# Half of the cross-attention probabilities carried through DRAM and transposed in 32x32 blocks by VectorE

## The reference

```python
qh = _split_heads(einsum('bnq,qi->bni', x, Wq))        # (8, 2048, 128)
kh = _split_heads(einsum('bmc,ci->bmi', context, Wk))  # (8, 4096, 128)
vh = _split_heads(einsum('bmc,ci->bmi', context, Wv))
sim = einsum('hid,hjd->hij', qh, kh) * SCALE
mean = mean(sim, axis=-1, keepdims=True)
sim = (sim - mean) * 1.5 + mean
attn = softmax(sim, axis=-1)
out = einsum('hij,hjd->hid', attn, vh)                 # then the heads side by side
return einsum('bni,iq->bnq', out, Wout) + bout
```

## Time and profile before

| | us |
|---|---|
| median of 3 runs | 2606.53 (2606.34 to 2611.48) |
| span of the profiled execution | 2603.9 |
| one ordinary step of the cross-attention | 30.79 |

### The profile page before, as it was taken

How to read it: one execution, slowest core, us unless ns; L and a number is a source line. 1 busy time by engine, 2 the same in 40 slices (tenths; PEclk the granted TensorE clock), 3 DMA queues, 4 the chain that set the end, 5 groups by cost and what they waited for, 6 DMA issues and landing times. The chain is left out here.

```text
span 2603.9 us, 47026 instructions
## 1 busy us (share of the span) xinstructions
PE 2543.7 (98%) x17647; PEld 2283.5 (88%) x17647; DVE 1914.2 (74%) x3606; ACT 1606.5 (62%) x3049; POOL 158.2 (6%) x208
## 2 busy tenths in 40 slices
PE   8999989999999999999999999999999999999998
PEld 6899868998899889988999899988998899889987
DVE  5888767776777677767777777767776777677787
ACT  6899646555666555565566466656665566556566
POOL 1344220000000000000000000000000000000003
PEclk9999999999999999999999999999999999999999
DMA  8765350001100120011000300020001200110001
GB/s 246 211 162 147 101 221 25 17 17 65 66 17 25 57 74 17 16 66 65 25 16 15 116 17 16 17 108 31 17 17 57 74 17 16 65 68 17 28 1 33
DMA packets 60638, 155.47 MB, mean 60 GB/s; under 512 B 8849, under 2 KB 22353, under 8 KB 60465
## 3 DMA queue, kind: packets, MB, share of 16 engines
q1 hardware_dynamic: 56464, 140.15, 16.7%
q0 software_dynamic: 3248, 12.72, 1.6%
q10 hardware_dynamic: 752, 0.26, 0.0%
HBM read 125.70 MB, written 27.39 MB: 59 GB/s over the span
## 5 line engine op out<-in xcount | busy, mean ns | idle before, releaser
L1731 ACT CAST pt_hi<-xt_ps 128x512 fp32r<-128x512 f32 x1024 | 592.4, 585 | 568.9 <-PE xt_ps L1698 553.0
L1810 DVE TENSOR_TENSOR pt_lo<-xt_ps,pt_hi 128x512 fp32r<-128x512 f32 x1024 | 704.4, 688 | 255.4 <-ACT pt_hi L1731 252.1
L1799 DVE TENSOR_SCALAR_CACHE_REDUCE xprobs<-xs_ps 128x1024 f32<-128x1024 f32 x512 | 626.6, 1224 | 176.1 <-PE xs_ps L1638 171.4
L1709 PE MATMUL xo_ps<-pt_hi,v_hi 128*128 128x256 f32 x2048 | 647.3, 316 | 2.4 <-DVE pt_lo L1810 2.3
L1737 ACT ACTIVATE xprobs<-xprobs,xneg_max 128x1024 f32<-128x1024 f32 x512 | 591.4, 1155 | 27.2 <-DVE xneg_max L1805 27.2
L1698 PE MATMUL xt_ps<-ident,xprobs 128*128 128x128 f32 x4096 | 603.7, 272 | 0.0
L1709 PE MATMUL xo_ps<-pt_hi,v_lo 128*128 128x256 f32 x2048 | 571.3, 279 | 0.0
L1709 PE MATMUL xo_ps<-pt_lo,v_hi 128*128 128x256 f32 x2048 | 570.0, 278 | 0.0
L1698 PEld LDWEIGHTS xt_ps<-ident,xprobs 128*128 128x128 f32 x4096 | 484.1, 140 | 61.9 <-issue 6.7
L1709 PEld LDWEIGHTS xo_ps<-pt_hi,v_hi 128*128 128x128 f32 x2048 | 386.3, 189 | 5.7 <-DVE pt_lo L1810 2.6
L1709 PEld LDWEIGHTS xo_ps<-pt_lo,v_hi 128*128 128x128 f32 x2048 | 388.3, 190 | 2.0
(11 more groups left out here) (251 smaller groups left out, 2736.3 us busy)
## 6 DMA issues: line engine op xcount, KB each, us to landing
v_split<-ctx_split SPq DMA_DIRECT2D x68, 768.0 KB, 5.8
xq<-x_split SPq DMA_DIRECT2D x64, 512.0 KB, 3.2
q_st<-rel_split SPq DMA_DIRECT2D x32, 256.0 KB, 3.8
q_st<-q_split SPq DMA_DIRECT2D x32, 192.0 KB, 4.6
k_st<-k_split SPq DMA_DIRECT2D x32, 192.0 KB, 4.7
ctx_split<-ctx_out POOLq DMA_DIRECT2D x8, 768.0 KB, 4.1
q_split<-attn_late SPq DMA_DIRECT2D x8, 512.0 KB, 4.0
k_split<-attn_late SPq DMA_DIRECT2D x8, 512.0 KB, 5.5
```

Source lines behind the costliest of these rows:

```text
L1709: last = pe.matmul(o_ps[:, 0:GQ], v[:, vs], pt[:, c % 3, GQ * j:GQ * (j + 1)], start=c == 0 and j == 0 and m == 0, stop=c == PIECES - 1 an ...
L1731: act.copy(pt_hi[:, c % 3, :], t_ps[:, c % 3, :]).then_inc(t_rounded, 1)
L1799: dve.tensor_scalar(probs[:, par if kind == "A" else 1 - par, t, CHUNK * i:CHUNK * (i + 1)], s_ps[:, buf, :], LOGIT, None, ALU.mult, ALU.m ...
L1810: dve.tensor_tensor(pt_lo[:, c % 3, :], t_ps[:, c % 3, :], pt_hi[:, c % 3, :].bitcast(F32), ALU.subtract).then_inc(t_ready, 1)
```

## The change

Of the 16 pieces of a step 8 are still transposed by TensorE ("T"), and 8 are carried ("D"). Their order is given by a string, one letter a piece. Keys are stored in another order, so that the carried half is the first plane of `probs` (`probs[:, 0]`), and each D piece consists of the same keys after the new way of transposing. Twice per group, when the exponentials of a tile are done, SP stores the carried half of that tile to a DRAM buffer `carried`, in four DMAs of 256 KB, each from 32 partitions in runs of 2 KB. Once both tiles are stored, it loads them back as `landed`, in four DMAs of 512 KB in runs of 512 B. After that the 32x32 blocks lie where they belong, and only their inside has to be transposed. That is one VectorE instruction in place for each piece (item "X"). ScalarE rounds the piece from `landed` to `pt_hi`, and GpSimd takes the rest to `pt_lo` and increments `d_ready`, for which TensorE's W of that piece waits.

`probs` gets a third plane, so that the half that TensorE transposes has two planes in turn while the carried half has one. VectorE therefore waits before it overwrites the carried plane of a tile until that tile is stored (`carried_out`). SP's loop over heads is written out, and its load of queries for the group after next stands between the two stores. At the end of the cross-attention GpSimd's work for the channel mix ("pn", "prest") is laid between its new subtractions. Semaphores are merged (`dve_self`, `pool_filled`, `x2_stored`), without another order of the work.

```diff
+ORDER = "TTTTDTDTDDTDDTDD"
+def flip_ahead(k):
+    ahead = [k + 1] if k + 1 < PIECES and ORDER[k + 1] == "D" else []
+    own = [k] if ORDER[k] == "D" and (k == 0 or ORDER.index("D") == k) else []
+    return [("X", piece_at(n)) for n in own + ahead if n in own or n != ORDER.index("D")]
...
     for c in range(PIECES):
-        items.append(("T", c))
+        flips = flip_ahead(c)
+        if ORDER[c] == "D" and ORDER.index("D") == c:
+            items.append(flips.pop(0))
+        items.append((ORDER[c], c))
+        items += flips
         if c >= 2:
             items.append(("W", c - 2))
...
+            def carry_out(s, t):
+                sp.wait_ge(exped, 2 * s + t + 1)
+                rows = carried[s % 2].rearrange("(g j) r c -> j g r c", g=QUADS)
+                for q in range(QUADS):
+                    sp.dma_start(rows[:, :, QUADS * t + q, :], probs[QUAD * q:QUAD * (q + 1), 0, t]).then_inc(carried_out[t], 16)
+            def carry_in(s):
+                for t in range(2):
+                    sp.wait_ge(carried_out[t], 16 * QUADS * (s + 1))
+                for m in range(GROUPS):
+                    if s:
+                        sp.wait_ge(d_ready, CARRIED * (s - 1) + 2 * (m + 1))
+                    sp.dma_start(landed[:, m], carried[s % 2][:, :, P * m:P * (m + 1)]).then_inc(carried_in[m], 16)
...
+                    elif kind == "X":
+                        p = item[1]
+                        dve.wait_ge(carried_in[p // 2], s * 16)
+                        dve.transpose(landed_piece(p), landed_piece(p)).then_inc(flipped, 1)
...
+                    elif kind == "D":
+                        k, p = item[1], piece_at(item[1])
+                        act.wait_ge(flipped, s * CARRIED + (p + 1 - CARRIED))
+                        if k >= 3:
+                            act.wait_ge(weighed, s * (PIECES - 1) + (k - 2 - (PIECES - 1)))
+                        act.copy(quads(pt_hi[:, k % 3, :]), landed_piece(p)).then_inc(d_rounded, 1)
...
+                    if kind == "D":
+                        k, p = item[1], piece_at(item[1])
+                        pool.wait_ge(d_rounded, s * CARRIED + (p + 1 - CARRIED))
+                        pool.tensor_tensor(quads(pt_lo[:, k % 3, :]), landed_piece(p), quads(pt_hi[:, k % 3, :]).bitcast(F32),
+                                           ALU.subtract).then_inc(d_ready, 1)
...
-                        pe.wait_ge(t_ready, s * PIECES + (c + 1 - PIECES))
+                        if ORDER[k] == "D":
+                            pe.wait_ge(d_ready, s * CARRIED + (p + 1 - CARRIED))
+                        else:
+                            pe.wait_ge(t_ready, s * TURNED + (turned_before(k) + 1 - TURNED))
...
+                        if i == 0 and items is not BEFORE:
+                            dve.wait_ge(carried_out[t], (s if kind == "A" else s - 1 if items is AFTER else s + 1) * (16 * QUADS))
```

More of the change, by code:

```diff
@@ L51 @@
 CHUNK = 1024
+QUAD = 32
+QUADS = P // QUAD
+ROWS = 2 * QUADS
 def flat(ap):
@@ L1225, in _, with __init__ @@
             keep_clock(6)
+    return streams.chain.n
 class ChannelMix:
-    def __init__(self, nc, ctx, a, x, v_split, keys, probs, small):
+    def __init__(self, nc, ctx, a, x, v_split, keys, probs, small, dve_self, chained):
         def sb(name, shape, dt=F32):
@@ L1444, in run_heads, with cross_attention @@
         head(h, h == XH - 1)
-def cross_attention(nc, a, x, ident, x2_split, x2_stored, k_shift, streams, keys, probs, mix):
+def cross_attention(nc, a, x, ident, x2_split, x2_stored, k_shift, streams, keys, probs, landed, carried, mix):
     with ExitStack() as ctx:
@@ L1523, in _ @@
             streams.load_blocks(sp, 3)
-            for g in range(1, G):
-                sp.wait_ge(x2_stored[g], 16)
+            for u in range(4):
+                sp.wait_ge(x2_stored[u], 32)
             sp.wait_ge(q_ready, 1)
@@ L1570, in _ @@
-            with sp.Fori(0, XH - 1) as h:
-                head(h, False)
-            head(XH - 1, True)
+                    streams.load_kv(sp, h * XD + XD)
+                    streams.load_wq(sp, h * XD + XD)
+                sp.dma_start(wo_raw[:], a["XWout"][bass.ds(h * XD, XD), :]).then_inc(wo_loaded, 16)
+                for g in range(G):
+                    s = h * G + g
+                    carry_out(s, 0)
+                    if g + 2 < G or (g + 2 == G and not last):
+                        sp.wait_ge(q_ready, s + 2)
+                        load_queries((g + 2) % G)
+                    if g == G - 1 and not last:
+                        used(STEP_7, ("K+", 0), STEP_AT[G - 1])
+                        streams.load_blocks(sp, 2)
+                    if g == G - 2 and last:
+                        mix.load_weights(sp)
+                    carry_out(s, 1)
+                    if g == G - 1 and not last:
+                        used(STEP_7, ("K+", 1), STEP_AT[G - 1])
+                        streams.load_blocks(sp, 3)
+                        sp.wait_ge(q_ready, s + 2)
+                        load_queries(1)
+                    carry_in(s)
@@ L1574, in _ @@
+                if not last:
+                    used(STEP_8, ("V+", 5), STEP_AT[G])
+                    streams.load_blocks(sp, 0)
+                    used(AFTER, ("V+", 6), AFTER_AT)
+                    streams.load_blocks(sp, 1)
+            for h in range(XH):
+                head(h, h == XH - 1)
         @block.gpsimd
@@ L1690, in run @@
                     elif kind == "T":
-                        c = item[1]
+                        c, own = turned_before(item[1]), probs[:, 2 - par]
                         if c == 0:
@@ L1777, in run @@
                     elif kind == "own":
+                        for t in range(2):
+                            act.wait_ge(carried_out[t], 16 * QUADS * XH * G)
                         act.wait_ge(filled, chunk + n)
```

201 lines of the change are left out of this document (107 added, 94 removed).

## The result

The changed kernel takes 2546.4 us (median of 4 runs, 2543.0 to 2550.0) against 2607.5 us before (now the median of 4 runs, 2606.3 to 2611.5): the ratio is 0.9766, with a 95% interval from 0.9752 to 0.9780. The change gains 61 us where 147 were forecast. The profiled execution has a span of 2541.3 us, before 2603.9.

A forecast was written before the change was run, and what follows sets the result against it. TensorE, busy 98% of the span, bounds the kernel. 64 x (3.5 - 1.0) = 160, less 9 for late transfers and 4 for normalisations, gives 147 us: 2606.5 becomes 2460 us, range 2390 to 2620.

The forecast's parts named there:

- rival B: Chain of a D piece dearer, less than the gain: GpSimd at 1.72 us gives 2536, block transposes of 1.09 2582; chance 0.15.
- 8 x 0.44 = 3.5 us a step: TensorE, each of 64 steps: 8 of 16 T pieces go, 0.44 us each; floor 27.3 us, at most 225 us gained.
- Block transpose 0.69, GpSimd subtraction 1.28, cast 0.61: Durations in us taken per carried piece on VectorE, GpSimd and ScalarE, from rows of the earlier profile.
- Waits of 1.0 us in an ordinary step: TensorE waits for the D pieces' chain 1.0 us a step, making a step of 28.3 us.
- W4: TensorE's W of piece 4, a D piece: can start at 4.7 us after T3's start, 0.3 us of waiting.
- W12: TensorE's W of piece 12, a D piece: can start at 6.3 us after T10's start, 0.5 us of waiting.
- 64 x (3.5 - 1.0): All 64 cross-attention steps: 3.5 us of transposes saved less 1.0 us of waiting each, 160 us.
- 1.1 late eight times, 9 us in all: Store and load of the carried half take 10 us: on time in ordinary steps, 1.1 us late at eight head changes.
- SP has nothing urgent behind its new waits: SP's DMA queue: the queries it loads are for the group after next, so the new waits delay nothing urgent.
- The granted clock should stay at 1.00; no wait that I expect is over 1.5 us: Whole kernel: clock stays at 1.00, no expected wait over 1.5 us; TensorE's waits for `pt_lo` about 60 us in total.
- Rivals C and D: Both slower: block transpose dear, 1.61 us, 2800 us, chance 0.12; transfers late, past 13.6 us, 2760 us, chance 0.09.
- D's mild form: Transfers landing after 11.1 us stop VectorE before the first block transpose; still faster below 13.6 us; rival's whole chance 0.09.

The follow-up runs named there:

- E1: Changed kernel without the carried half's stores, loads, block transposes, casts and subtractions; TensorE only weighs what stands in the buffers; output not the reference's: 2387.8 us.
- E8: Changed kernel with E5's order and lead, E6's earlier context blocks, and four GpSimd normalisations moved ahead of the last step's subtractions: 2428.6 us, ratio 0.9314.
- E2: Changed kernel without stores and loads of the carried half; block transposes, casts and subtractions work on constants; output not the reference's: 2507.6 us.
- E6: Changed kernel with the second pair of context blocks issued before the second tile's four stores at the change of heads: 2537.5 us, ratio 0.9734.
- E3: Changed kernel with half of each GpSimd subtraction left out, 128x256 instead of 128x512; output not the reference's: 2483.2 us.
- E4: Changed kernel with every block transpose but a step's first issued two pieces ahead instead of one: 2531.0 us, ratio 0.9711.
- E9: Changed kernel with E5's order of pieces, but every block transpose only one piece ahead: 2524.2 us, ratio 0.9678.
- E5: Changed kernel with piece order TTTTTDDTDDDTTDDD and block transposes two pieces ahead, a step's first one piece ahead: 2443.8 us, ratio 0.9371.

## Why the prediction was wrong

It forecast the sign and the mechanism, and a gain of 147 us; 61 came. The measured time lies in the band of rival B ("the chain of a D piece is dearer"), but not for B's reasons: both durations that B doubted came as forecast. Step by step:

- **"8 x 0.44 = 3.5 us a step", a floor of 27.3 us: right.** E1 has 27.35. Over the whole kernel 220 us instead of 225.
- **Block transpose 0.69, GpSimd subtraction 1.28, cast 0.61: right**, with 0.70, 1.30 and 0.62. The estimate that the prediction made from the Trainium skill ("VectorE: DVE Perf Modes", The three transpose paths) was 0.71 us, and the trace agrees with 0.70. The table of the same page of the Trainium skill, Rules for kernel authors, by which one transposes 128x128 on TensorE where PSUM will do, isn't borne out by this case: with TensorE as the bound, half of them on VectorE gains 2.3%, and 6.9% once they are well placed (E8).
- **Waits of 1.0 us in an ordinary step: close**, 1.3 to 1.4 (E1 against E2 and after). W4 was 0.4 late instead of 0.3, W12 0.4 instead of 0.5. W8 (0.2, one of the six "on time by 0 to 0.5 us") is what the sum had as its margin (1.0 for 0.8 laid out). Not counted was 0.1 us more in the W after each stop. With the floor 0.05 higher than read, the miss is 40 x 0.45 = 18 us.
- **"64 x (3.5 - 1.0)": this is the step that failed.** The waits of an ordinary step were multiplied by 64, but only 40 steps are ordinary. The other 24 have other work around the chain: the weights' casts in the first one, the projections of keys and values at the change of heads, which stand in front of a carried piece's cast in one place and leave TensorE less to do beside the chain in another, no scores at all at the end. There E2 less E1 shows 17, 36 and 15 us where the sum had 8, 14 and 6 (its 4 us for the normalisations among them). Together with the transfers, of which next, these steps account for 67 of the 85 us that were missed. The earlier trace rows holds one ordinary step, and of the other kinds of step the prediction read nothing but one time in the earlier trace rows.
- **The late load "1.1 late eight times, 9 us in all": the transfer was right, its price wrong.** From the stores' issue to the load's it took 6.4 us and then 4.4 to land (means of eight heads), where 6 and 4 were taken. VectorE was 0.95 to 2.6 us late in the eight heads, 1.8 in the mean. But the wait goes on to TensorE with nothing to absorb it, and in four of the eight heads the clock fell to half after it, for 1.3 us more. E2 puts the price at 8 x 2.5 = 20 us.
- **"SP has nothing urgent behind its new waits": wrong.** This holds for the queries. The second pair of context blocks at the change of heads stands in the same queue, and E6 shows 9 us for it by the times (2546.4 - 2537.5), of which its windows over the change of heads have 5.
- **"The granted clock should stay at 1.00; no wait that I expect is over 1.5 us": wrong.** The wait for the first carried piece of a head was over 1.5 us in seven of eight heads, 3.0 at most, as were three waits in the last two steps, and the clock fell to half in four heads. TensorE's printed waits for `pt_lo` are 84 us in total, where 60 were expected.
- **Rivals C and D didn't come**: no instruction was dear, and no transfer was 13.6 us behind its exponential in an ordinary step. D's mild form was there in the first step of each head.

## What to carry to other kernels

A sum over steps wants one row from each kind of step. Where a new chain through several engines hides behind other work, the steps with different work around it (the first, the last, the change from one outer iteration to the next) have to be laid out one by one, since there the cover is thinner and the queues hold something else. Before an operation is made shorter, its place and its lead should be tried: here nothing but order and lead took the step from 28.75 to 27.4 us, and either of them alone only to 28.6. A new wait on a DMA queue is charged to whatever transfer stands behind it, so all that follows in that queue has to be read, not only the next item. And where the clock moves, stretches are compared at the same granted clock: E3's means alone would have said that a shorter GpSimd hop does little at the change of heads.

## What the runs showed of the hardware

**The clock after a short stop.** The granted clock fell to 0.50 behind TensorE's stop of 1.98 us shown above, and the window of that step reads 0.95. So it was in heads with stops of 2.94, 1.74 and 1.78 us too. In the others, with 1.21, 1.81, 2.49 and 3.01 us, it stayed at 1.00. The length of one stop doesn't decide it, then; what does can't be told from these runs. It costs 1.3 us each time (TensorE busy for 29.2 to 29.3 us against 27.8 to 28.0 in that step). In E3, E4 and E9 the clock also fell in three of the seven changes of heads, in the changed kernel in none.

**The clock at the end.** In the last two steps TensorE stops often, and the clock can be lower in work behind them that the change doesn't touch. From the last W to the end of the kernel the changed kernel, E2, E5 and E8 read

```profile
2490.59:2541.31 50.72, 39.93 (x273) 36.59 (x271) 38.39 (x62) 30.02 (x55) 20.40 (x15) 0.97 0.13 42
```

```profile
2455.85:2505.80 49.95, 38.83 (x273) 35.41 (x271) 38.98 (x62) 29.97 (x55) 20.63 (x15) 0.99 0.13 43
```

```profile
2390.39:2444.00 53.61, 42.94 (x272) 38.81 (x271) 38.48 (x62) 30.06 (x55) 19.93 (x14) 0.88 0.12 40
```

```profile
2375.69:2428.20 52.51, 41.84 (x273) 38.00 (x271) 38.36 (x62) 30.08 (x55) 20.42 (x15) 0.93 0.12 41
```

with the same instructions: 49.95 us at a clock of 0.99, 50.72 at 0.97, 52.51 at 0.93, 53.61 at 0.88. In E5 3.7 us of what the end lost are therefore lost in the channel mix, at a lower clock; in the changed kernel, whose end lost 7.9 us, it is 0.8. Of the 5 us by which E8's end is shorter than E5's, 1.1 are this. That the stops in front of it bring the clock down isn't shown: E2 waits as long for GpSimd in its last two steps as the changed kernel (11.0 and 11.1 us) and keeps 0.99.

**Block transposes of 4-byte elements** run at 0.70 us for 128x512 in place, and neither they nor the 164 GB/s of traffic stretched the GpSimd subtractions of the ordinary steps (1.28 to 1.32 us).
